# Local transformers in another form: a stream kept skewed by one token, query norms in the exponential, other engine orders

## The reference

```python
x = x + _L0_ffn_ref(_layernorm(x, axis=-1), L0_ffn_Wqkv, ...)
...
def shift_tokens(t):                     # channels 64..127 come from the token before
    a, s = jnp.split(t, 2, -1)
    s = jnp.pad(s, ((0, 0), (1, 0), (0, 0)))[:, :-1]
    return jnp.concatenate([a, s], -1)
...
q = l2norm(q) * qs
k = l2norm(k) * ksc
q = q * cos * scale + rotate_half(q) * sin * scale
...
sim = jnp.einsum('bhwie,bhwje->bhwij', bq, bk2) * QK_SCALE
sim = jnp.where(mask, -jnp.finfo(sim.dtype).max, sim)
attn = jax.nn.softmax(sim, -1)
out = jnp.einsum('bhwij,bhwje->bhwie', attn, bv2)
...
hg = xn @ W1 + b1                        # 128 -> 2 x 341
a, gate = jnp.split(hg, 2, -1)
return a * jax.nn.gelu(gate, approximate=False) @ W2 + b2
...
for i in range(DEPTH):
    x = attn_layer(shift_tokens(x), Wqkv[i], q_scale[i], k_scale[i], Wo[i]) + x
    x = ffn_layer(shift_tokens(x), ln_g[i], ln_b[i], W1[i], b1[i], W2[i], b2[i]) + x
```

## Time and profile before

| | |
|---|---|
| median of three runs | 4326.34 us |
| the profiled execution: time, span | 4323.92 us, 4321.8 us |
| busy: PE, DVE, ACT, POOL | 3978.9, 3553.1, 3383.5, 3444.7 us |
| busy share: PE, DVE, ACT, POOL | 92%, 82%, 78%, 80% |
| costliest groups | exponentials 1002.7 us, GpSimd's sums of rotary parts 974.1 us, projections 810.3 us |

### The profile page before, as it was taken

One profiled execution on the slowest core, in us unless ns is written; L12 is line 12 of the kernel. 1 busy time (PEld: TensorE's weight loads), 2 busy tenths in 40 slices (PEclk: granted clock), 3 DMA queues, 4 the chain that ended last, 5 costly groups with the idle time before them and its releaser, 6 DMA issues. The chain is left out here.

```text
span 4321.8 us, 141652 instructions
## 1 busy us (share of the span) xinstructions
PE 3978.9 (92%) x52427; PEld 2331.2 (54%) x52427; DVE 3553.1 (82%) x11447; ACT 3383.5 (78%) x10657; POOL 3444.7 (80%) x4293
## 2 busy tenths in 40 slices
PE   6888799999999999999767999999999999996686
PEld 2333356665665665656453665665655666653464
DVE  6999788888888888888376888888888888874646
ACT  5888489999999999999415999999999999982122
POOL 3999788988988998898297988998898898871323
PEclk8999899999999999999888999999999999997788
DMA  1000110111111111011002011111111111100000
GB/s 28 1 1 1 46 32 24 42 39 29 41 37 41 29 44 37 24 39 27 11 0 61 24 37 42 27 51 30 33 46 29 41 30 36 29 24 3 5 3 10
DMA packets 78612, 122.77 MB, mean 28 GB/s; under 512 B 26024, under 2 KB 47204, under 8 KB 77924
## 3 DMA queue, kind: packets, MB, share of 16 engines
q1 hardware_dynamic: 77924, 113.71, 10.2%
HBM read 35.56 MB, written 1.05 MB: 8 GB/s over the span
## 5 line engine op out<-in xcount | busy, mean ns | idle before, releaser
L1371 ACT ACTIVATE local_pr<-local_tb,local_nmax 128x96 f32<-128x96 f32 x3072 | 1002.7, 356 | 190.4 <-DVE local_nmax L1507 179.9
L1082 POOL TENSOR_TENSOR local_qk<-local_qk,local_rb 128x512 f32<-128x512 f32 x768 | 974.1, 1280 | 131.9 <-DVE local_rb L1491 131.3
L1185 PE MATMUL local_pj<-local_wqkv,local_xs 128*64 128x512 f32 x3072 | 810.3, 606 | 27.9 <-DVE local_rb L1491 14.0
L1088 POOL TENSOR_TENSOR local_qk<-local_qk,local_rinv 128x512 f32<-128x512 f32 x768 | 791.9, 1047 | 7.5
L1507 DVE CUSTOM_DVE_ANT_0 local_tb<-local_tb,local_mask 128x96 f32<-128x96 f32 x3072 | 680.1, 292 | 6.9 <-PE local_tb L1210 6.9
L1371 ACT ACTIVATION_READ_ACCUMULATOR local_pr<-local_tb,local_nmax 128x1 f32 x3072 | 683.6, 223 | 0.0
L1498 DVE TENSOR_REDUCE local_ss<-local_sq 128x8 f32<-128x512 f32 x768 | 522.2, 680 | 155.5 <-ACT local_sq L1354 142.7
L1109 POOL TENSOR_TENSOR local_pr<-local_pr,local_rsum 128x384 f32<-128x384 f32 x768 | 623.5, 829 | 32.1 <-DVE local_rsum L1513 32.1
L1488 DVE TENSOR_TENSOR local_qk<-local_pj,local_rope 128x512 f32<-128x512 f32 x768 | 516.7, 673 | 50.4 <-ACT local_sq L1354 41.9
L1354 ACT ACTIVATE local_sq<-local_pj 128x512 f32<-128x512 f32 x768 | 487.8, 635 | 51.6 <-PE local_pj L1185 45.5
L1491 DVE TENSOR_TENSOR local_rb<-local_pj,local_rope 128x512 f32<-128x512 f32 x768 | 523.1, 681 | 0.0
(11 more groups left out here) (421 smaller groups left out, 7429.8 us busy)
## 6 DMA issues: line engine op xcount, KB each, us to landing
local_v<-local_v SPq DMA_DIRECT2D x288, 256.0 KB, 3.8
local_wqkv<-L_ffn_Wqkv_dram SPq DMA_DIRECT2D x72, 256.0 KB, 2.8
local_wo<-L_ffn_Wo_dram SPq DMA_DIRECT2D x12, 512.0 KB, 4.1
local_w<-L_ffn_W_dram SPq DMA_DIRECT2D x12, 341.0 KB, 3.7
mamba_parts<-mamba_in_low SPq DMA_DIRECT2D x24, 64.0 KB, 2.0
local_w<-L_ffn_W_dram SPq DMA_DIRECT2D x12, 128.0 KB
y_dram<-store_xtok SPq DMA_DIRECT2D x4, 256.0 KB, 2.8
local_oT<-rope_dram SPq DMA_DIRECT2D x2, 256.0 KB, 2.7
```

The source lines that it names most:

```text
L1082: nc.gpsimd.tensor_tensor(qk[:, u, :], qk[:, u, :], rb[:, u % 2, :], ALU.add).then_inc(s["summed"], 1)
L1088: nc.gpsimd.tensor_tensor(heads8(qk[:, u, :]), heads8(qk[:, u, :]), r, ALU.mult).then_inc(s["scaled"], 1)
L1185: ins = nc.tensor.matmul(bank[own, :], xs[:, par, u // 4 * P + own.start:u // 4 * P + own.stop], wqkv[:, dep % 2, u % 4 * BANK:(u % 4 + 1) ...
L1371: ins = nc.scalar.activation(pr[:, (NU * c + k) % PR_RING, i, WIN:WIN + KW], scores[:, i * KW:(i + 1) * KW], ACT.Exp, scale=-1.0, bias=nma ...
```

## The change

The stream is kept skewed: rows 64 to 127 of each sequence stand one column further on, in 257 columns, and this is what the projections and the centring read. The shifted copies go. Output projection and W2 write 257 columns, each half reading its operand one column shifted against the other; b2 becomes a row of W2 with a row of ones in g; the final product of the normalisation writes the skewed form in halves. W1 is padded so that its last tile has 64 columns. Queries are no longer scaled on GpSimd: VectorE multiplies minus the maximum by the query's 1/norm (`bias`, eight a sequence, 128x4), and the exponential gets the norm as its scale. Only the four key units are scaled. The diagonals are made on GpSimd in one 128x256 product. All lists are new, with the `tb` and `pj` rotations that go with them; the output projection moves from lag 5 to 6, projection and norms to lags 2 and 3, part of the scores and values from 4 to 5.

```diff
@@ Net, normalise @@
-        self.zT = root.sb("zT", [P, B, L])
+        both = root.sb("zT", [P, B * (L + 1)])
+        self.zT = both[:, 0:B * L].rearrange("p (b l) -> p b l", b=B)
+        self.skewed = both[:, :].rearrange("p (b l) -> p b l", b=B)
...
-                nc.vector.tensor_tensor(part(z, q), part(z, q), p_bc[:, q, :], ALU.mult)
+                if skewed:
+                    own = BANK // L
+                    for rows, first in ((slice(0, P // 2), 0), (slice(P // 2, P), 1)):
+                        nc.vector.tensor_tensor(net.skewed[rows, own * q:own * (q + 1), first:first + L], part(z, q)[rows, :].rearrange("p (b l) -> p b l", l=L),
+                                                p_bc[rows, q, :].rearrange("p (b l) -> p b l", l=L), ALU.mult)
+                else:
+                    nc.vector.tensor_tensor(part(z, q), part(z, q), p_bc[:, q, :], ALU.mult)
@@ local_transformer: loads, constants @@
-        w1 = m.sb("w1", [P, 2 * DIN])
+        w1 = m.sb("w1", [P, DIN + 3 * P])
-        oT = m.sb("oT", [P, PAIRS, L])
+        oT = m.sb("oT", [P, PAIRS, L + 2])
+            sp.dma_start(w2[FT[2]:FK[2], 2, :], d["L0_ffn_b2"][k:k + 1, :]).then_inc(s["w2_in"], 16)
...
+            nc.vector.memset(g[HALF:P, 2, 1:L + 1], 1.0)
+            nc.vector.memset(w1[:, 2 * DIN:DIN + 3 * P], 0.0)
@@ GpSimd @@
-                r = view(rinv[:, u * 8:(u + 1) * 8], [[1, 8], [0, DH]])
+                r = view(rinv[:, a % ROOT_RING, u * 8:(u + 1) * 8], [[1, 8], [0, DH]])
+            def spread_root(e, par, _):
+                pool.wait_ge(s["std_ready"], e + 1)
+                need(pool, s["spread"], e)
+                nc.gpsimd.tensor_tensor(diag[:, :, :], view(net.ident[:, 0:1], [[0, 2], [1, P]]), view(deviation[:, 0:1], [[1, 2], [0, P]]),
+                                        ALU.mult).then_inc(s["diag_ready"], 1)
@@ TensorE @@
-                    ins = nc.tensor.matmul(bank[own, :], xs[:, par, u // 4 * P + own.start:u // 4 * P + own.stop],
+                    ins = nc.tensor.matmul(bank[own, :], stream[:, a % B, u // 4 * P + own.start:u // 4 * P + own.stop],
-                pe.wait_ge(s["scaled"], QK_UNITS * b + 2 * j + 2)
+                if j % 2:
+                    pe.wait_ge(s["scaled"], len(K_UNITS) * b + j + 1)
+                else:
+                    pe.wait_ge(s["summed"], QK_UNITS * b + 2 * j + 2)
-                        ins = nc.tensor.matmul(fb[own, 0:L], wo[:, j, own], oT[:, j, :], start=(j == 0), stop=(j == INNER // P - 1),
+                        ins = nc.tensor.matmul(fb[own, 0:L + 1], wo[:, j, own], oT[:, j, 1 - h:L + 2 - h], start=(j == 0), stop=(j == INNER // P - 1),
-                    ins = nc.tensor.matmul(fb[own, 0:L], net.center[:, own], xs2[:, :], start=True, stop=True, skip_group_check=True)
+                    ins = nc.tensor.matmul(fb[own, 0:L], net.center[:, own], z1[:, par, 0:L], start=True, stop=True, skip_group_check=True)
-                    for low, high in ((0, HALF), (HALF, FT[j])):
-                        ins = nc.tensor.matmul(fb[low:high, i * L:(i + 1) * L], w1[:, half * DIN + j * P + low:half * DIN + j * P + high], xn[:, :],
+                    for own in COLUMNS:
+                        first = half * DIN + j * P
+                        ins = nc.tensor.matmul(fb[own, i * L:(i + 1) * L], w1[:, first + own.start:first + own.stop], xn[:, :],
-                        ins = nc.tensor.matmul(fb[own, 0:L], w2[0:FT[j], j, own], g[0:FT[j], j, :], start=(j == 0), stop=(j == 2), skip_group_check=True)
+                        ins = nc.tensor.matmul(fb[own, 0:L + 1], w2[0:FK[j], j, own], g[0:FK[j], j, 1 - h:L + 2 - h], start=(j == 0), stop=(j == 2),
@@ ScalarE @@
-                act.wait_ge(s["maxed"], NU * c + k + 1)
+                act.wait_ge(s["biased"], NU * c + k + 1)
-                scores = pair_of_banks("score", k // 2)[k % 2]
+                scores, norms = pair_of_banks("score", k // 2)[k % 2], query_norms(c, k)
-                                               scale=-1.0, bias=nmax[:, k, i:i + 1], accum_out=esum[:, k // 2, k % 2, i:i + 1])
+                                               scale=norms[:, i:i + 1], bias=nbias[:, k, i:i + 1], accum_out=esum[:, k // 2, k % 2, i:i + 1])
-            def spread_std(e, par, _):
-                act.wait_ge(s["std_ready"], e + 1)
-                need(act, s["spread"], e)
-                for t in range(2):
-                    ins = nc.scalar.activation(diag[:, t, :], net.ident[:, :], ACT.Copy, scale=deviation[:, t:t + 1])
-                ins.then_inc(s["diag_ready"], 1)
@@ VectorE @@
-            def shift_in(n, par, _):
...
-                    ins = nc.vector.tensor_tensor_reduce(at, at, mask[:, k // 4, :], -1.0, 3.0e38, ALU.add, ALU.min, nmax[:, k, i:i + 1])
+                    ins = nc.vector.tensor_tensor_reduce(at, at, mask[:, k // 4, :], 1.0, -3.0e38, ALU.add, ALU.max, smax[:, k, i:i + 1])
+            def bias(c, par, k):
+                dve.wait_ge(s["maxed"], NU * c + k + 1)
+                dve.wait_ge(s["root_steps"], ROOT_ALL * c + ROOT_ALL)
+                need(dve, s["exped"], NU * (c - 1) + k + 1)
+                nc.vector.scalar_tensor_tensor(nbias[:, k, :], smax[:, k, :], -1.0, query_norms(c, k), ALU.mult, ALU.mult).then_inc(s["biased"], 1)
-                for own, to, count in ((slice(0, h), 0, L), (slice(h, C), 1, L - 1)):
-                    nc.vector.tensor_tensor(xs2[own, to:to + count], z[own, e % B, 0:count], fb[own, 0:count], ALU.add).then_inc(s["xs2_ready"], 1)
-                nc.vector.tensor_tensor(z1[:, e % 2, :], z[:, e % B, :], fb[:, 0:L], ALU.add).then_inc(s["z1_ready"], 1)
+                nc.vector.tensor_tensor(z1[:, par, :], stream[:, e % B, 0:L + 1], fb[:, 0:L + 1], ALU.add).then_inc(s["z1_ready"], 1)
-                nc.vector.scalar_tensor_tensor(z[:, f % B, :], fb[:, 0:L], cols[:, f // B, 6:7], z1[:, f % 2, :],
-                                               ALU.add, ALU.add).then_inc(s["z_ready"], 1)
+                nc.vector.tensor_tensor(stream[:, f % B, 0:L + 1], z1[:, par, :], fb[:, 0:L + 1], ALU.add).then_inc(s["z_ready"], 1)
@@ the order lists (one of five, its first entries) @@
-                run(square, 3, 2)
-                run(copy_qk, 4, 4)
...
+                run(square, 3, 5)
+                run(exps, 5, 1)
```

More of the change, by code:

```diff
@@ L819 @@
 POOL_STEPS = 1 + 3 * 4
+ROOT_RING = 4
+K_UNITS = (2, 3, 6, 7)
 V_BLOCK = (3, 0, 2, 1)
@@ L1024, in couple, with query_norms @@
             return kk // 2, kk % 2
+        def query_norms(c, k):
+            t, half = couple(k // 2)
+            first = (4 * t + half) * 8 + k % 2
+            return rinv[:, c % ROOT_RING, first:first + 7:2]
         ROOT_ALL = 1 + POOL_STEPS
@@ L1195, in project_v @@
                 for own in COLUMNS:
-                    ins = nc.tensor.matmul(bank[own, :], xs[:, par, j // 2 * P + own.start:j // 2 * P + own.stop],
+                    ins = nc.tensor.matmul(bank[own, :], stream[:, b % B, j // 2 * P + own.start:j // 2 * P + own.stop],
                                            wqkv[:, dep % 2, col:col + BANK], start=True, stop=True, skip_group_check=True)
@@ new lines, in iteration @@
+                run(score, 5, 2)
+                run(project_v, 5, 3)
+                run(weigh, 6, 3)
+                run(out_project, 6, 0)
+                run(out_project, 6, 1)
+                run(turn_probs, 5, 0)
+                run(project, 2, 0)
+                run(centre, 6, 0)
+                run(turn_qk, 3, 0)
+                run(score, 5, 3)
+                run(project_v, 4, 0)
+                run(variance, 6, 0)
+                run(project_v, 4, 1)
+                run(project, 2, 1)
@@ new lines, in iteration @@
+                run(rotate, 3, 7)
+                run(residual1, 6, 0)
+                run(rotate, 2, 0)
+                run(maxima, 5, 6)
+                run(add_eps, 6, 0)
+                run(bias, 5, 6)
+                run(maxima, 5, 7)
+                run(bias, 5, 7)
+                run(sum_squares, 2, 0)
+                run(recip, 5, 2)
+                run(rotate, 2, 1)
+                run(affine, 6, 0)
+                run(rotate, 2, 2)
+                run(sum_squares, 2, 1)
+                run(copy_o, 5, 0)
```

357 lines of the change are left out of this document (168 added, 189 removed).

## The result

The changed kernel takes 4558.5 us (median of 4 runs, 4557.0 to 4560.9), the kernel before on the same chip 4323.3 us: a ratio of 1.0544, 95% interval [1.0526, 1.0562]. It is slower, as forecast, but by 235 us and not by 88: the time lies outside the range too. The profiled execution has a span of 4555.8 us against 4321.8 before.

The account below looks back on a forecast made before the run. TensorE bounds the kernel at 32.6 us a period; afterwards ScalarE would, at 31.4 plus 2.1 of waits, 33.5. Over 92 periods that adds 83 us, plus 5 of normalisation: 4323.9 becomes 4412 us, range 4366 to 4467.

Parts of the forecast that it names:

- The sign and the mechanism: Whole kernel: 2.0% slower, as the exponential's scale column costs 0.097 us each and ScalarE takes over as the bound.
- up parts: TensorE's FFN instruction groups: the two with the 21-column tile fall from 1.60 and 1.49 to 0.87 us, saving 1.3.
- ScalarE's own work: ScalarE per period: 28.9 us, less 0.6 for diagonals, plus 3.1 for 32 exponentials with a scale column, is 31.4.
- 2.1 us of waits.: ScalarE's waits per period in the new order: 1.6, 0.3 and 0.2 us, added to its 31.4.
- three walked waits: ScalarE waits 1.6 us before the copy of v, 0.3 before couple 3's exponentials, 0.2 before the third gelu.
- In draining 0, give or take 8: Stage ends: FFN chain 1.3 us a sequence shorter, last turn, copy and probability product about 3 us longer; net 0.
- some six iterations of filling: Stage starts: about six iterations fill and four drain each stage, leaving 92 steady periods; no filling cost was added.
- What lies outside: Normalisation before each local stage: four products become eight half-height ones, 4.8 us in both stages, taken as 5.
- 3.7 us a period: ScalarE in the kernel before: 28.9 us of work in a 32.6 us period, so this much counted as spare.
- Faster: Rival: the exponential's scale column costs nothing or is hidden, TensorE's 31.45 us decides, total 4223; 0.16 for this side.
- Slower than forecast: Rival: VectorE's eight bias products cost 0.3 us, not 0.1, ScalarE loses 0.8 more: period 34.3, total 4486; chance 0.17.
- Shifted halves: Rival: TensorE's halves reading shifted columns do not overlap, adding 4.6 us a period: 36.05, total 4646; chance 0.03.

Follow-up runs that it names:

- e3: Kernel before with only the last tile of W1 padded from 21 to 128 columns (zeros): 4217.3 us, ratio 0.9753 to before.
- e1: Changed kernel with the exponentials' scale the number 1.0, not a column of norms (computation incomplete): 4313.7 us, ratio 0.9972 to before.
- e2: Kernel before with the exponential's scale read from a memory column holding -1.0, not the number -1.0: 4514.8 us, ratio 1.0438 to before.
- e10: Changed kernel with the scale from memory on two of four exponentials per block, 1.0 on the others (computation incomplete): 4423.1 us, ratio 1.0232 to before.
- e5: Changed kernel in the old orders, queries scaled on GpSimd, exponential's scale -1.0, no bias products: 4222.4 us, ratio 0.9770 to before.
- e7: Changed kernel with ScalarE's last copy of v moved behind the next exponentials: 4577.9 us, ratio 1.0590 to before.
- e12: Changed kernel with TensorE's last projection of v moved ahead of the second score couple: 4544.4 us, ratio 1.0513 to before.
- e9: Changed kernel with VectorE's bias product replaced by minus the maximum alone, one input (computation incomplete): 4554.1 us, ratio 1.0532 to before.

## Why the prediction was wrong

**The sign and the mechanism were right.** TensorE's up parts fell to 0.87 us, the one before another tile shape to 0.96 (e3: 1.14 for 1.3 us a period). The exponential grew by 97 ns, 354 to 451, and by 93 from start to start. ScalarE's own work, added up as in the prediction, is 31.48 us for 31.4 forecast. GpSimd is at 75.5% for 77. VectorE's bias takes 0.27 us on average, inside its bounds of 0.1 to 0.3. e1, e2 and e10 show that the operand is the cost. The gain that it hides is 12 us with all the rest of the change (e1), and 101 without the new orders and the bias products (e5).

**Two terms of the sum were wrong.**

*"2.1 us of waits."* They are 2.97, and the period 34.45 for 33.5: 0.95 x 86 intervals is 82 us of the 146 by which the profiled execution's 234 us exceed the 88 forecast. The three walked waits were near: 1.73 for 1.6, 0.40 for 0.3, 0.17 for 0.2. Not walked were 0.35 us before another block of exponentials (behind its bias on VectorE), and 0.17 and 0.13 at the table loads and their neighbours. I had stopped at three places of the order instead of going once round. VectorE's and ScalarE's timelines show the 0.35:

```profile
1050.74 0.36 DVE L1533 SCALAR_TENSOR_TENSOR local_nbias<-local_smax,local_rinv 128x4 f32<-128x4 f32 x1
```

```profile
1051.14 0.43 ACT L1409 ACTIVATE local_pr<-local_tb,local_nbias,local_rinv 128x96 f32<-128x96 f32 x1 [0.36 <-DVE local_nbias L1533]
```

This bias product takes 0.36 us where it takes 0.15 with GpSimd still, and ends at 1051.10 beside a GpSimd sum that ends at 1051.09 (started at 1048.58, two of them in 2.51). As an estimate from these two durations, some 0.2 of the 0.35 us is that wait, which the prediction did not have.

*"In draining 0, give or take 8", and the filling not worked out at all.* The prediction counted "some six iterations of filling" as equal in both kernels. It knew from the lists that the output projection moves from lag 5 to 6, and took that for a matter of the drain. The way of a sequence grew from 4.01 to 4.76 periods, and the first result of each stage came 22 and 24 us later: 46 us. The last four intervals add 13, and the additions to the residual, in halves since the stream is skewed, 1.5 us more than before on three intervals a stage, 9 us. What lies outside is 9 for 5. Against these stands that I counted 92 even periods where there are 86, which takes off 5.

*Behind the first of the two: idle time of ScalarE is not spare.* The prediction gave the kernel before 3.7 us a period of it. e2 puts 3.0 us of work into it and the period grows by 2.0: 2.7 us of waits stay. In the new orders 3.5 us stay when ScalarE has 28.5 us of work (e1), 3.1 with 30 (e10) and 3.0 with 31.5, and a wait removed at one place comes back at the next (e7, e12). By the rows of waits the time passes in a loop through ScalarE's exponentials, TensorE's turns, scores and projections, and VectorE's maxima; that is read from them and not shown by a run of its own. Why this loop has about 3 us of waits was not taken apart, and no order was tried that makes it shorter. That cause stays open.

**The rivals.** "Faster" (operand free) is refuted by the 451 ns of the changed kernel's exponentials and by e10's rows. Its own total was off as well: e1 has the period without the price, and takes 4313.7 us where the rival had 4223, with 31.97 for 31.45 us a period and 34 us more of filling. "Slower than forecast" (4486) came nearest, with a period of 34.3 for 34.45, and had VectorE's bias at 0.3 us right. Its 0.8 us more of waits are in part luck: only some 0.35 of them stand behind a bias that was not walked, and in the total it misses the filling too. "Shifted halves" is refuted by e5. Small slips of the sums change nothing: one more column on 22 passes is 0.02 us by the 0.87 us of four passes of 256, not 0.04, and two of the rivals' totals are off by 1 us.

## What to carry to other kernels

Work added to an engine that is 93% busy beside a full neighbour cost two thirds of itself in the old orders (2.0 of 3.0 us) and five sixths in the new (2.5), and moving a wait (e7, e12) did not remove it; count as spare only what an experiment puts in without moving the period. A form of instruction that saves work on an engine that is not the bound (GpSimd here) and lengthens 32 small ones on a nearly full one is a bad trade, and it can hide a gain: the padded tile alone was worth 2.5%. For a software pipeline work out two numbers, the period and the way of one item in periods; the second is paid at each stage's beginning. Here it cost 46 us of 234, and no view of the even part shows it.

## What the hardware showed beyond that

Some VectorE instructions stand still while a GpSimd product runs. Over the changed kernel's two stages, bias products (128x4) that began at least 0.15 us before the end of a running GpSimd instruction took 454 ns on average, the others 152; of the 16 pairs of 64x256 additions the first took 1.27 us in eight, all beside a GpSimd product, and the other 24 additions 0.42. Both kinds read two tensors of SBUF; in e9 the one-input `tensor_scalar` took 462 ns beside and 160 otherwise. It does not hold for every instruction on SBUF: the sums of squares (L1516) took 677 ns beside a running GpSimd instruction and 668 otherwise, the reciprocals (L1538) 194 and 194. A small product placed just behind such an operation is priced by what is left of it.
